# Two value groups and two units of maxima of the projection are run inside the attention's first slot

## The reference

```python
q = _lin(_lin(x, wq_w, wq_b), vq_w, vq_b)
k = _lin(_lin(x, wk_w, wk_b), vk_w, vk_b)
v = _lin(_lin(x, wv_w, wv_b), vv_w, vv_b)
q = q.reshape(b, s, hc, H).transpose(2, 0, 1, 3)   # hc = 32 heads of H = 16
...
scores = jnp.einsum('cbqh,cbkh->cbqk', q, k) / scale
attn = jax.nn.softmax(scores, axis=-1)
o = jnp.einsum('cbqk,cbkh->cbqh', attn, v)
...
x = _layernorm(x + attention);  x = _layernorm(x + gated convolution);  x = _layernorm(x + quantised linear)
```

## Time and profile before

| | us |
|---|---|
| median of 3 runs | 2084.42 |
| lowest, highest | 2068.49, 2117.22 |
| the profiled execution | 2066.98 |
| its span, first to last instruction | 2065.3 |
| TensorE, DVE, ScalarE, GpSimd busy | 2020.9, 1640.8, 1328.1, 487.3 |

### The profile page before, as it was taken

The page is one execution under the profiler, slowest core; times in us unless marked ns, Lnnn a source line. Parts: engine busy times, 40 slices in busy tenths (PEclk is TensorE's granted clock), DMA queues, the critical chain, the costliest instruction groups (busy, mean ns, idle before and its releaser), DMA issues.

```text
span 2065.3 us, 43069 instructions
## 1 busy us (share of the span) xinstructions
PE 2020.9 (98%) x12800; PEld 1155.1 (56%) x12800; DVE 1640.8 (79%) x1727; ACT 1328.1 (64%) x2429; POOL 487.3 (24%) x878
## 2 busy tenths in 40 slices
PE   9999999999999999999999999999999999999996
PEld 4788776444444444444444444444444487767774
DVE  4333356999999999999999999999999467886787
ACT  0111113888888888888888888888888733453344
POOL 0000001112212211221122122112212452574245
PEclk9999999999999999999999999999999999999997
DMA  4465835566785765766665756657667679763672
GB/s 168 134 171 147 203 98 123 86 132 136 109 143 128 114 135 100 142 136 106 132 138 109 139 130 111 138 105 135 135 110 194 217 251 333 269 234 128 227 266 93
DMA packets 214416, 315.28 MB, mean 153 GB/s; under 512 B 105424, under 2 KB 121808, under 8 KB 202064
## 3 DMA queue, kind: packets, MB, share of 16 engines
q1 hardware_dynamic: 214352, 314.47, 63.5%
HBM read 211.06 MB, written 101.19 MB: 151 GB/s over the span
## 4 chain that ended last, share of the span: by engine, by line
PE 89%; DVE 6%; ACT 2%; POOL 1%; issue 1%; DMA 1%; SPq 1%; POOLq 0%; DVEq 0%; ACTq 0%
PE psum L187 24%; PE psum L559 23%; PE psum L584 15%; PE psum L223 14%; PE psum L595 10%; PE psum L88 2%; DVE stats L1477 1%; PE psum L1397 1%; DVE y L1602 1%; ACT probs L701 1%; DVE gates L1576 1%; DVE gates L1573 1%; ACT gates L1326 1%; DMA x_block<-in_x_t_dram 0%; DVE y L1507 0%
## 5 line engine op out<-in xcount | busy, mean ns | idle before, releaser
L230 DVE TENSOR_REDUCE neg_max<-psum 128x1 f32<-128x1024 f32 x1024 | 1191.2, 1217 | 98.2 <-PE psum L223 82.6
L701 ACT ACTIVATE probs<-psum 128x512 f32<-128x512 f32 x2048 | 1071.5, 601 | 192.3 <-PE psum L559 187.1
L559 PE MATMUL psum<-q_op,k_op 50*128 50x512 f32 x2048 | 659.5, 454 | 0.1
L223 PE MATMUL psum<-k_op,q_op 48*128 48x512 f32 x2048 | 616.3, 486 | 0.8 <-DVE neg_max L230 0.8
L559 PEld LDWEIGHTS psum<-q_op,k_op 50*128 50x128 f32 x2048 | 310.2, 190 | 448.1 <-ACT probs L701 440.3
L223 PEld LDWEIGHTS psum<-k_op,q_op 48*128 48x128 f32 x2048 | 387.9, 315 | 26.4 <-DVE neg_max L230 11.2
L584 PE MATMUL psum<-probs,v_op 128*32 128x512 f32 x2560 | 341.8, 606 | 3.7 <-ACT out L690 0.7
L187 PE MATMUL psum<-x_wino,conv_w 128*128 128x512 f32 x1152 | 275.7, 395 | 0.0
L595 PE MATMUL psum<-probs,v_op 128*32 128x256 f32 x3072 | 245.4, 391 | 0.5 <-ACT probs L701 0.5
L187 PEld LDWEIGHTS psum<-x_wino,conv_w 128*128 128x128 f32 x1152 | 214.5, 188 | 45.7 <-issue 0.2
L241 POOL CAST neg_max_parts<-neg_max 128x8 fp32r<-128x8 f32 x128 | 24.3, 190 | 726.6 <-DVE neg_max L230 726.6
(11 more groups left out here) (105 smaller groups left out, 1705.7 us busy)
## 6 DMA issues: line engine op xcount, KB each, us to landing
q_op<-qk_parts_dram SPq DMA_DIRECT2D x384, 128.0 KB, 4.8
conv_w<-conv_w_parts_dram SPq DMA_DIRECT2D x32, 1536.0 KB, 6.8
qk_parts_dram<-qk_parts SPq DMA_DIRECT2D x128, 256.0 KB, 3.2
k_op<-qk_parts_dram SPq DMA_DIRECT2D x384, 64.0 KB, 5.2
conv_w_parts_dram<-conv_w_parts SPq DMA_DIRECT2D x16, 1536.0 KB, 7.0
attended_dram<-out SPq DMA_DIRECT2D x64, 256.0 KB, 3.8
attended_parts_dram<-o_parts SPq DMA_DIRECT2D x128, 128.0 KB, 3.1
gates<-in_ctx_dram SPq DMA_DIRECT2D x32, 512.0 KB, 7.6
```

Of the source, the lines that this page charges most:

```text
L223: return nc.tensor.matmul(mem["pair"][t % 2][:, lane * HALF:(lane + 1) * HALF], ops["q"][i][r, b, t:S:QT], ops["k"][i][r, b, :], start=Tru ...
L230: nc.vector.tensor_reduce(ops["max"][b][:, t:t + 1], mem["pair"][t % 2][:], AX_X, ALU.max, negate=True).then_inc(ops["maxed"], 1)
L559: nc.tensor.matmul(score_bank(k, t, last), kop[k][r, j // 2, n // 2 * P:(n // 2 + 1) * P], qop[k][r, j // 2, j % 2 * HALF:(j % 2 + 1) * HALF],
L701: nc.scalar.activation(probs[n % DEEP][:, c ^ n % 2, :], score_bank(k, t, last), ACT.Exp, scale=SCALE).then_inc(exp_done, 1)
```

## The change

The last two of the last block's value groups (`KEPT = 2`) and the last two lead units (22 and 23) leave the projection. TensorE runs them in the attention's first slot: each kept group in two blocks of 6 matmuls into bank 7, between the slot's first scores and units. DVE evacuates them there (`kept_out`) between the maxima of 22 and 23 and behind that of unit 25. The waits at the start of `attend` ask for two groups less on TensorE, SP and GpSimd; TensorE waits for the kept evacuations before the value product v0 of every fourth slot. The tiles that the kept groups read (the second x block's two parts, the third weight's two parts, the value bias) are laid out where the attention's first tiles don't overwrite them.

```diff
+KEPT = 2
@@ project, PE and DVE
-                    for j in range(GROUPS):
+                    for j in range(GROUPS - (KEPT if units and i == 1 else 0)):
...
-                for j in range(GROUPS):
+                for j in range(GROUPS - (KEPT if blk == BLK - 1 else 0)):
@@ attend, SP, PE, POOL
-            sp.wait_ge(proj, PROJECTED)
+            sp.wait_ge(proj, PROJECTED - KEPT)
...
-            pe.wait_ge(v_out, 4 + PROJECTED // 3)
+            pe.wait_ge(v_out, 4 + PROJECTED // 3 - KEPT)
...
-            pool.wait_ge(proj, PROJECTED)
+            pool.wait_ge(proj, PROJECTED - KEPT)
@@ attend, PE, values()
                     pe.wait_ge(pv_out, s + 1)
+                    if k == 0:
+                        pe.wait_ge(v_out, 4 + PROJECTED // 3)
@@ attend, PE
+            def lead_unit(n, lane):
+
+                pe.wait_ge(maxed, n - 1)
+                b, t = n // QT % 2, n % QT
+                score_lane(nc, mem, ops, n // 16, b, t, lane)
+                score_lane(nc, mem, ops, n // 16, b, t, 1 - lane).then_inc(s1_full, 1)
+
+            def kept_values(m, kcs):
+
+                if m > 0 and kcs[0] == 0:
+                    pe.wait_ge(v_out, 4 + PROJECTED // 3 - KEPT + m)
+                cols = slice((KC - KEPT + m) * P, (KC - KEPT + m + 1) * P)
+                mm = product3(nc, pv_bank, [(kept["xh"][:, kc, cols], kept["xl"][:, kc, cols],
+                                             kept["wh"][:, kc, :], kept["wl"][:, kc, :]) for kc in kcs],
+                              kcs[0] == 0, kcs[-1] == KC - 1)
+                if kcs[-1] == KC - 1:
+                    mm.then_inc(proj, 1)
@@ attend, PE, slot()
+                if first and k == 0:
+                    shifted(it, k, 0, last)
+                    shifted(it, k, 1, last)
+                    kept_values(0, (0,1))
+                    lead_unit(LEAD - 2, 0)
+                    shifted(it, k, 2, last)
+                    kept_values(0, (2,3))
+                    lead_unit(LEAD - 1, 1)
+                    shifted(it, k, 3, last)
+                    unit(it, k, 0, 0, last)
+                    kept_values(1, (0,1))
+                    unit(it, k, 1, 0, last)
+                    kept_values(1, (2,3))
+                    unit(it, k, 2, 0, last)
+                else:
...
@@ attend, DVE
+                    if first and k == 0 and n in KEPT_OUT:
+                        kept_out(1)
+
+            def kept_out(m):
+
+                dve.wait_ge(proj, PROJECTED - KEPT + m + 1)
+                nc.vector.tensor_tensor(
+                    kept["values_of"][:, :, 1, :, 4 * KC - KEPT + m, :], pv_bank.rearrange("p (g h d) -> p g h d", g=2, d=DH),
+                    kept["bias"].rearrange("p (g h d) -> p g h d", g=2, d=DH), ALU.add).then_inc(v_out, 1)
+
+            max_of_unit(nc, dve, mem, ops, 0, QT - 2, LEAD - 2)
+            kept_out(0)
+            max_of_unit(nc, dve, mem, ops, 0, QT - 1, LEAD - 1)
```

More of the change, by code:

```diff
@@ L397, in _, with attend @@
                 split_max(nc, pool, ops, n // 2, n % 2, n, n * QT + QT)
-def attend(nc, block, sem, mem, qk_scr, v_sb, us_scr, r_scr, on_scr, cw_scr, wo_t, conv_w, x_nat, wo_b, tern_t, norm, late, ops, proj, qk_lo, v_out):
+def attend(nc, block, sem, mem, qk_scr, v_sb, us_scr, r_scr, on_scr, cw_scr, wo_t, conv_w, x_nat, wo_b, tern_t, norm, late, ops, proj, qk_lo, v_out, kept):
     STEPS = QT
@@ L407, in attend @@
     TURN = 8
+    KEPT_OUT = (1,)
     EVACUATE_AFTER = 3
@@ L606, in values_before @@
                         values(s - 1, (k - 1) % 4, n)
[L608 to L616, removed]
+                if first and k == 0:
[13 more added lines that the diff above has]
+                else:
+                    shifted(it, k, 0, last)
+                    unit(it, k, 0, 1, last)
+                    values_before(6)
+                    shifted(it, k, 1, last)
+                    unit(it, k, 1, 0, last)
+                    shifted(it, k, 2, last)
+                    shifted(it, k, 3, last)
+                    unit(it, k, 2, 0, last)
+                    values_before(7)
                 shifted(it, k, 4, last)
@@ L1663, in build @@
                 sb = lambda name, shape, dt: weights.enter_context(nc.sbuf_tensor(name, shape, dt))
-                w_hi = [sb(f"w_hi{s}", [P, KC, F], F32R) for s in range(3)]
-                w_lo = [sb(f"w_lo{s}", [P, KC, F], F32R) for s in range(3)]
+                second = [sb(f"x_{part}1", [P, KC, HALF], F32R) for part in ("hi", "lo")]
+                w_hi, w_lo = [[sb(f"w_{part}{s}", [P, KC, F], F32R) for s in range(2)] for part in ("hi", "lo")]
                 qk_bias = sb("qk_bias", [P, 2, KC], F32)
-                v_bias = sb("v_bias", [P, F], F32)
                 x = {
                     "raw": [sb(f"x_block{i}", [P, KC, HALF], F32) for i in range(2)],
-                    "hi": [sb(f"x_hi{i}", [P, KC, HALF], F32R) for i in range(2)],
-                    "lo": [sb(f"x_lo{i}", [P, KC, HALF], F32R) for i in range(2)],
+                    "hi": [sb("x_hi0", [P, KC, HALF], F32R), second[0]],
+                    "lo": [sb("x_lo0", [P, KC, HALF], F32R), second[1]],
                     "in": [sem(f"x_block_in{i}") for i in range(2)],
@@ L1675, in build @@
                     "made": sem("x_made"),
+                }
+                top = nc.sbuf_base + 4 * PARTS * HALF * 4
+                for part, w in (("hi", w_hi), ("lo", w_lo)):
+                    w.append(nc.alloc_sbuf_tensor_at(f"w_{part}2", [P, KC, F], F32R, offset=top))
+                    top += KC * F * 4
+                v_bias = nc.alloc_sbuf_tensor_at("v_bias", [P, F], F32, offset=top)
+                kept = {
+                    "xh": second[0], "xl": second[1], "wh": w_hi[2], "wl": w_lo[2], "bias": v_bias[:],
+                    "values_of": v_sb[:].rearrange("p a f -> p (a f)")
+                                 .rearrange("p (g b h t d) -> p g b h t d", g=2, b=2, t=2 * QT, d=DH),
                 }
@@ L1726, in build @@
                 attended = attend(nc, block, sem, mem, qk_scr, v_sb, us_scr, r_scr, on_scr, cw_scr, a["wo_t"], a["conv_w"], a["x"], a["wo_b"],
-                       a["tern_t"], norm, late, ops, proj, qk_lo, v_out)
+                       a["tern_t"], norm, late, ops, proj, qk_lo, v_out, kept)
                 finish(nc, block, sem, attended, mem, us_scr, r_scr, on_scr, cw_scr, norm, late, a["x"], a["ctx"], a["conv_b"],
```

## The result

| us | before | after |
|---|---|---|
| median, 15 runs each, taken in turns | 2082.46 | 2061.79 |
| lowest, highest | 2065.78, 2117.64 | 2058.64, 2064.03 |
| profiled execution, its span | 2066.98, 2065.3 | 2058.64, 2056.9 |

The ratio of the times is 0.9944, with a 95% interval of 0.9926 to 0.9963: 7.7 to 15.4 us less, within the 2% that I called no change, but clear of zero. The ratio leaves out executions that lie more than 1.5% over the fastest of the same kernel; the medians of all executions, 20.7 us apart, leave out none. The more striking thing is in the second row: the times of before spread over 52 us, those of after over 5.

What follows compares the result with a forecast made beforehand. TensorE, busy 98%, bounds the kernel. Seam terms 1.01 + 2.68 + 7.22 + 20.28 = 31.19 us are 3.91 under 35.10; less 0.8 of waits, 3.1 us gained: 2084.42 to 2081.3 us, range 2063 to 2105.

Steps and rivals of the forecast that it cites:

- The seam's sum: Units 20 and 21 to second v0: 1.01 + 2.68 + 7.22 + 20.28 = 31.19 us without waits, against 35.10 before.
- 0.8 of waits: In the first slot's new head TensorE waits about 0.8 us in all, bounds 0 and 2.86 us.
- The two lists side by side: TensorE's and DVE's orders in the new head, laid out together: DVE idles 0.5 and 0.6 us, TensorE sets the pace.
- The terms for the work and its switches: First slot's head: 2.68 us of its own work, 7.22 us of kept work with four pairs of matmul switches.
- The loads' step: Third-operand loads start at about 333.3 us instead of 339.82, land about 345.4, before the ninth unit's 349.6; no cost.
- The clock: At the seam the half clock, 1.68 us behind v0 and some of the head's 2.86, is taken as gone.
- The rule of the Trainium skill: Frequent micro-idles between matmul groups can swing the clock, so blocks between scores could keep the fall; then 2084.6 us.
- The term for the half clock: First v0 to second v0: half clock costs 21.96 - 20.28 = 1.68 us, from about 7 us at the lower level.
- The range is mostly that spread: Whole kernel: runs from 2068.49 to 2117.22 us lie far wider than any case, so the range is 2063 to 2105.
- 332.04 us ..., which no part of the change moves.: Start of units 20 and 21, where the seam's measurement begins, stays at 332.04 us under the change.
- 1 to 3: First-slot head: clock falls as before, 2084.6 us (0.14); DVE paces, 2083.4 (0.12); half clock through all blocks, 2090.4 (0.03).
- 4: Behind the seam: something it doesn't feed sets the pace and the 3 us return as waits; gain 0, chance 0.03.

Runs made afterwards that it cites:

- layout_only: The kernel before with only the changed kernel's placement of the projection's tiles in SBUF; median 2078.51 us, ratio 1.0057.
- x_early_unkept: The kernel before with the bias tile padded to 64 bytes and the x blocks loaded early, without the change; median 2071.55 us, ratio 0.9991.

## Why the prediction was right, and where it was not

**The seam's sum held.** I forecast 32.0 us (31.19 and 0.8 of waits); it took 31.76. The head from units 20 and 21 to v0: forecast 11.8, measured 11.46. From v0 to v0: 20.28, measured 20.30. The two lists side by side gave DVE's idle times as 0.5 and 0.6 us; they were 0.66 and 0.59. The waits of TensorE were over-priced: the 0.3 us before the third block did not open, as the evacuation ended at 334.80 and the block began at 335.03, behind a unit. That the total came out within 0.3 us is partly luck: no matmul of the head waited, so the 0.8 us of waits should have been 0, but from the first score (329.59) to v0 it took 10.45 us where the sum has 2.68 + 7.22 = 9.90. The terms for the work and its switches were 0.55 us too small, and the two errors nearly cancel.

**The loads' step held**, and mattered more than I gave it. The first was issued at 329.77, 1.19 us behind the start of units 20 and 21 (forecast 1.3). I had worked out that loads issued as before would land 2.3 us too late and then booked the edit at no cost; taking it away cost 5.3 us of idle time and the clock. About 3 of the 5.3 come from the later group that the loads then wait for, so the 2.3 fits.

**The clock held at 1.00**, as forecast. The rule of the Trainium skill that I set against it (page "TensorE: Matmul & The Clock Gate", section "A second HAM failure mode: psum-queue depth-cycling") did not decide here: with 1.62 us of idle ahead of the blocks the clock stayed up too.

**The size was wrong.** Forecast was a gain of 3.1 us; the ratio gives 7.7 to 15.4 us, the medians of all executions 20.7. The median of 2061.79 us lies 1.2 us under the range's lower end; in the ratio's terms (0.9944 times 2084.42, 2072.7) it lies inside. Three steps failed:
- The term for the half clock. "The half clock cost 21.96 - 20.28 = 1.68 us" took one execution's 6.8 us for a property of the kernel. Its length varies: the other two profiles have 20.5 us, and 5.4 to 5.6 us more of time. By 0.41 us per us, an estimate, 2.8 us of the profiled seam's 3.34 are half clock and 8.4 us of a 40.6 us seam. The rest would be DVE's waits; the seam of `layout_only`, with half of the first profile's half clock and the same length, says that this split is rough.
- "The range is mostly that spread": I carried the spread of 2068 to 2117 over to the changed kernel as noise. The profile before had its source in view, the one place where TensorE is at half clock in the attention, and I did not connect the two. With the fall gone the spread is 5 us, and the 15 executions of the changed kernel have mean clocks of 0.990 to 0.993, the 82 of the kernel before 0.963 to 0.992.
- "332.04 us ..., which no part of the change moves." The order of allocation moved it, by 3.5 us; the other differences ahead of it (a shorter stop at x block 6, a later start) cancelled to 0.04. I had read that part of the diff only for what overwrites what.

**The rivals.** 1 to 3 needed a fall of the clock or waits for DVE; neither came. 4 (the gain comes back as waits) did not come either: behind the second v0 1.60 us less were measured, 0.89 of them at a shorter half clock late in `finish`, the rest unexplained; the stretch of 1697 us is equal to 0.1%.

## What to carry to other kernels

When one kernel's times spread by 2% and its profile has one stretch at half clock, profile that stretch more than once, and set the mean granted clock of each execution beside its time: the stretch's length can be what spreads the times, and a profile of the shortest execution hides its price. Fill a seam with dense matmuls that have to be done anyway, and check for each wait that moves with them which load is released by it. When tiles are allocated in another order, compare the spacing of the same matmuls before and after; their addresses modulo 64 are a first thing to check, not a full rule.

## What the hardware showed

- A fall of TensorE's clock at the same place lasted 6.8, 20.5 and 20.5 us in three profiles of one kernel, each behind idle times of 0.51 and 0.27 us (a third one of 0.28 in the second); behind 5.3 us of idle it lasted 13.7 and 23.9 us. One us at half clock cost 0.41 us between two profiles of one kernel, 0.52 between two of another, and 0.43 over 82 executions; 0.5 would be the cost if all of the time went with the clock.
- Over 82 executions of one kernel the time follows the mean granted clock: 0.992 at 2063.5 us, 0.963 at 2118.9.
- 1.62 us of idle in 2.3 us, followed by 128-row matmuls, brought no fall. Single stops of 1.97 to 3.21 us among 128-row matmuls brought none in six profiles; stops of 3.03 to 4.83 us brought one of 3.4 or 6.8 us in six others.
- fp32r matmuls of 128 x 128 x 512 followed each other in 0.2333 us when the streamed and the loaded tile started 32 bytes apart modulo 64, and in 0.2267 us when they started alike in half of the groups: 3.7 us of the whole kernel. With all of them alike the others have 0.2287 to 0.2292 us, and in `x_early_unkept`, alike too, the value groups 0.233.
